# Moving two thirds of the last batch's shared upward products and batch 2's shared downward products behind the expert loop

## The reference, cut to what is computed

```python
router_logits = x @ gate_w.T
topk_w, topk_idx = jax.lax.top_k(softmax(router_logits), 6)      # of 64 experts
h = silu(einsum('th,eih->tei', x, experts_w1))                   # 176 wide
routed_out = sum over a token's 6 experts of weight * (h @ w2.T)
gu = x @ shared_gate_up.T ; g, u = split(gu, 2)                  # 352 wide each
shared_out = (silu(g) * u) @ shared_down.T
x = x + routed_out + shared_out
```

## Time and profile before

| | us |
|---|---|
| median of 3 runs (1401.63 to 1403.54) | 1402.77 |
| the profiled execution's own time | 1403.14 |
| its span | 1401.3 |
| PE busy | 1269.8 (91%) |
| DVE busy | 821.6 (59%) |
| ACT busy | 461.0 (33%) |
| POOL busy | 377.1 (27%) |

### The profile page before, as it was taken

The page is one execution under the profiler, slowest core; times in us unless marked ns, Lnnn a source line. Parts: engine busy times, 40 slices in busy tenths (PEclk is TensorE's granted clock), DMA queues, the critical chain, the costliest instruction groups (busy, mean ns, idle before and its releaser), DMA issues.

```text
span 1401.3 us, 19618 instructions
## 1 busy us (share of the span) xinstructions
PE 1269.8 (91%) x6002; PEld 813.4 (58%) x6002; DVE 821.6 (59%) x2227; ACT 461.0 (33%) x1038; POOL 377.1 (27%) x464
## 2 busy tenths in 40 slices
PE   5499999999999899998999999998177899899988
PEld 4256665555665556556568888886143546455454
DVE  1556776787578957794533333333468665776431
ACT  0255525553345425452211111111142432524310
POOL 0033203253334413361430000002457063330200
PEclk9799999999999999999999999999578999999999
DMA  9999999999800100012158777774222012000000
GB/s 310 413 415 409 410 408 408 409 400 386 335 1 23 69 1 1 8 64 86 62 163 238 224 227 228 229 225 134 68 64 72 1 46 61 23 23 15 1 16 15
DMA packets 107611, 234.40 MB, mean 167 GB/s; under 512 B 12400, under 2 KB 61200, under 8 KB 107152
## 3 DMA queue, kind: packets, MB, share of 16 engines
q1 hardware_dynamic: 80912, 191.50, 37.9%
q0 software_dynamic: 9216, 25.18, 5.6%
q10 hardware_dynamic: 17408, 16.78, 3.5%
HBM read 66.70 MB, written 166.72 MB: 167 GB/s over the span
## 4 chain that ended last, share of the span: by engine, by line
PE 71%; DVE 21%; issue 3%; ACT 2%; POOL 2%; DMA 1%; ACTq 0%; DVEq 0%; POOLq 0%; SPq 0%
PE bank L1234 8%; PE bank L1245 8%; PE bank L537 5%; PE bank L625 4%; PE bank L498 4%; PE bank L499 4%; PE bank L563 4%; PE bank L1476 3%; DVE negmax L839 3%; PE bank L1465 3%; DVE r L850 3%; PE bank L1459 3%; PE bank L546 3%; PE bank L1510 2%; PE bank L1620 2%
## 5 line engine op out<-in xcount | busy, mean ns | idle before, releaser
L697 ACT ACTIVATE r<-bank,negmax 128x128 f32<-128x128 f32 (+3 forms) x256 | 134.9, 527 | 173.8 <-DVE negmax L839 173.4
L537 PE MATMUL bank<-r 128*128 128x512 f32 (+3 forms) x512 | 184.3, 443 | 0.0
L839 DVE TENSOR_REDUCE negmax<-bank 128x1 f32<-128x128 f32 (+3 forms) x256 | 124.0, 485 | 41.5 <-PE bank L538 38.8
L934 POOL TENSOR_TENSOR r<-r,tables 128x256 f32<-128x256 f32 x56 | 42.1, 751 | 328.0 <-ACT r L680 327.8
L546 PE MATMUL bank<-tables,r 128*128 128x128 f32 x640 | 115.1, 278 | 12.2 <-DVE r L850 11.7
L1154 POOL DMA_INDIRECT w2buf<-sent,slots x48 | 49.6, 1034 | 280.5 <-ACTq L1290 258.7
L1234 PE MATMUL bank<-r 128*88 128x256 f32 x512 | 122.8, 383 | 1.9 <-DVE r L1301 1.9
L1146 POOL DMA_INDIRECT sent<-r,slots x96 | 94.0, 979 | 99.7 <-DVE slots L1074 40.0
L1245 PE MATMUL bank<-w2buf,r 88*128 88x256 f32 x512 | 118.5, 379 | 0.0
L546 PEld LDWEIGHTS bank<-tables,r 128*128 128x128 f32 x640 | 72.8, 141 | 66.0 <-DVE r L850 31.7
L1282 ACT ACTIVATE r<-bank 88x512 f32<-88x512 f32 x64 | 37.9, 592 | 219.7 <-PE bank L1234 219.7
(11 more groups left out here) (256 smaller groups left out, 2275.5 us busy)
## 6 DMA issues: line engine op xcount, KB each, us to landing
sent<-gath SPq DMA_DIRECT2D x8, 16384.0 KB, 95.8
r<-sent SPq DMA_DIRECT2D x64, 256.0 KB, 3.2
sent<-r ACTq DMA_DIRECT2D x64, 256.0 KB, 3.2
r<-w1T_dram SPq DMA_DIRECT2D x64, 176.0 KB
w2buf<-w2T_dram SPq DMA_DIRECT2D x64, 176.0 KB
r<-w_o_dram SPq DMA_DIRECT2D x1, 2048.0 KB, 14.2
x<-x_dram SPq DMA_DIRECT2D x1, 2048.0 KB, 19.7
out_dram<-x SPq DMA_DIRECT2D x4, 512.0 KB, 2.9
```

Of the source, the lines that this page charges most:

```text
L537: nc.tensor.matmul(at[:, 0:n], QT[g % 2][:, h, i * P:(i + 1) * P], KT[:, 0:n], start=True, stop=False)
L697: nc.scalar.activation(prob[:, u % 4, 0:(i + 1) * P], bank[SCORE[u % 4]][:, 0:(i + 1) * P], ACT.Exp, bias=negmax[:, u:u + 1], scale=1.0, a ...
L839: nc.vector.tensor_reduce(negmax[:, u:u + 1], bank[SCORE[u % 4]][:, 0:(i + 1) * P], axis=AX.X, op=ALU.max, negate=True).then_inc(A["max"], 1)
```

## The change

On every engine `shared_up/silu/hidden(3, (0, 1))`, `shared_down(2)` and `shared_add(2)` move from in front of the expert loop to behind it. On DVE they stand in front of the six `weigh`. PE gets a wait behind its loop for the last copy of the expert results (`M["ey"]`), since the downward products of batch 2 write banks 4 and 5, and `shared_down(3)` loses its wait on `R["trips"]`, which had come long before.

```diff
             with pe.Fori(0, last_it) as it:
                 step(it, True)
             step(last_it, False)
+            hold(pe, "pe", M["ey"], LT4 * last_it + LT4 + START)
...
             for i in range(TB):
-                if b == BATCH - 1 and i < 2:
-                    pe.wait_ge(R["trips"], 1)
-                else:
+                if b < BATCH - 1 or i >= 2:
                     need(pe, M["sacc"], TB * b + i - 1)
...
             shared_silu(act, 2, (0, 1, 2))
-            shared_silu(act, 3, (0, 1))
             experts_scalar(act)
-            shared_silu(act, 3, (2,))
+            shared_silu(act, 3, (0, 1, 2))
...
             shared_add(dve, 1)
-            shared_hidden(dve, 3, (0, 1))
-            shared_add(dve, 2)
             route.shares(c)
             route.portions(c)
             experts_vector(dve)
+            shared_hidden(dve, 3, (0, 1))
+            shared_add(dve, 2)
             for k in range(TOPK):
                 route.weigh(c, k)
             shared_hidden(dve, 3, (2,))
...
             shared_down(pe, 1)
+            experts_tensor(pe)
             shared_up(pe, 3, (0, 1))
             shared_down(pe, 2)
-            experts_tensor(pe)
             shared_up(pe, 3, (2,))
             shared_down(pe, 3)
```

## The result

The changed kernel takes 1407.82 us (median of 6 runs, 1405.9 to 1409.14) against 1403.62 us (1401.63 to 1404.1, 6 runs) beside it: a ratio of 1.0031, 95% interval 1.002 to 1.0042. It is 4.2 us slower. The profiled execution has a span of 1405.6 us, 4.3 us more than before.

What follows compares the result with a forecast made beforehand. Sends and loads, not PE, set the expert loop's start; behind it POOL's gathers run with 3.1 us of DVE slack. -0.3 + 4.4 + 0.9 = +5.0 us on 1403.14 us, less 0.37 us for the median: 1407.8 us, range 1404.8 to 1411.0 us.

Steps and rivals of the forecast that it cites:

- The front: Before the expert loop: weights limit the gain to 0.6 us, clock costs 0.3 us; -0.3 us, between -1.9 and +0.7.
- Clock at the front: First upward products at the loop's start: PE's idleness costs 0 to 1.3 us more at low clock; 0.3 us taken.
- The loop: Inside the expert loop: nothing added between turns, SP's queue unchanged; zero.
- The new wait: PE behind the loop: waits for the last expert result's copy, until 969.05 us against 968.06 us before; 1.0 us.
- The weighings behind the adds: DVE behind the loop: weighings follow the moved adds, delaying tile 0's return and POOL's third gather group; +4.4 us.
- over 4 us: Sign in the profile after: POOL waits over 4 us for DVE before the third group of gathers.
- Batch 3's downward products: PE behind the loop: first half at low clock, 8.2 us, delays tile 1's return and the fourth gather group; +0.9 us.
- both halves slow: Batch 3's downward products, both halves as slow as before (10.0 us): +2.9 us, used in the clock rival.
- The clock decides: Rival: PE keeps the low clock in both short stretches, in front and behind; +8.0 us, 1410.8 us; chance 0.20.
- Early experts: Rival at PE's loop start: rows could load some 12 us earlier; -6.8 us, 1396 us; chance 0.05.
- Paid back: Rival: front yields its whole 1.92 us wait, clock stays up for batch 3's downward products; +2.5 us, 1405.3 us; chance 0.13.

Runs made afterwards that it cites:

- run 2: Run 1's kernel with DVE's return of tile 0 put ahead of the last chunk's hidden product; ratio 1.0003 to the kernel before.
- Run 3: Kernel before, with DVE's shares and portions ahead of the last batch's hidden products and batch 2's adds, nothing moved behind the loop; ratio 0.9999.
- Run 5: Run 2's kernel with as many unused filler matmuls on PE in front of the loop as were moved away; ratio 0.9999 to the kernel before.
- run 11: Kernel before with portions early and expert weights issued ahead of the wait for the sends, repeated on a chip without stalls; ratio 0.9981.
- run 1: Changed kernel with DVE's six weighings put ahead of the moved hidden products and adds; ratio 1.0002 to the kernel before.
- run 4: Changed kernel with a third gather buffer, so POOL's third group waits for nothing, DVE's order kept; ratio 1.0001 to the kernel before.
- run 8: Run 2's kernel with SP issuing the first four tiles' expert weights before waiting for the sends; ratio 0.9996 to the kernel before.
- run 6: Run 5's kernel with 80 already met waits on PE in place of the filler matmuls; ratio 1.0003 to the kernel before.
- run 12: Run 5's kernel with the weights issued ahead of the wait for the sends, repeated on a chip without stalls; ratio 0.9988 to the kernel before.

## Why the prediction was right, point by point

*The time.* 1407.8 us forecast, 1407.82 us measured. That the two agree so closely is luck. The effect was forecast at +5.0 us and is +4.2 us, since a term of 0.9 us came to nothing, and the kernel before happened to come out 0.85 us higher in the six runs than in the three. What was right is the mechanism: without that term the sum is +4.1 us.

*The front, -0.3 us.* Measured -0.39 us in the profile. Its main reason held: PE's work was hidden (11.78 us of idle time ended by the rows). The weights are what comes last in runs 2 and 3 (1.44 and 1.64 us); in the changed kernel's own trace it is the copy behind the slow transposes (0.83 us), so there the low clock took part of the gain directly. Run 3 shows that even DVE's part of the gain was nearly nothing.

*Clock at the front, 0.3 us.* I took the 3.64 us of the first product for what a short pause always costs. Run 5 had it at 1.96 us after 0.77 and 1.39 us of pauses, run 11 at 3.53 us after 1.02 and 0.76 us, which is less in all. So the length of the pauses alone does not decide it. What does is not shown, and my term was one draw of it.

*The loop, 0.* Held: from the start of the second upward product to the last copy it is 246.51 us (968.75 - 722.24) against 246.44 us.

*The new wait, 1.0 us.* 0.97 us, and it passes on only through DVE's queue: in run 2 PE has the same wait, and POOL waits for nobody.

*The weighings behind the adds, +4.4 us.* This is the step that carries the result. The return of tile 0 ended at 991.65 us (forecast 991.3 us). Measured from the last copy, the third group of gathers starts 4.57 us later than before (991.91 - 968.75 against 986.95 - 968.36). Runs 1, 2 and 4 take it away. But the POOL wait is 3.08 us, less than the "over 4 us" I named, because the first gather was itself 1.9 us late, of which I had nothing. The late store does not add to the 4.57 us, which DVE sets; once POOL hardly waits for DVE any more, in runs 1, 2 and 4, it is what is left.

*Batch 3's downward products, +0.9 us.* Mis-sized: the products took 7.10 us, not 8.2, and the return of tile 1 ended at 996.18 + 3.10 = 999.28 us, just when POOL had finished its third group. POOL's wait there is 0.30 us, the length of its ordinary pause between two gathers. The term is 0. There is also a slip in my sum for both halves slow: 988.2 + 10.0 = 998.2 us, last add 998.6 us, return 1001.7 us against 999.0 us is +2.7 us and not +2.9 us, so the rival of the clock stands at 1410.6 us.

*The rivals.* "The clock decides" did not come: the first product lost to the clock what it had lost before (3.71 and 3.64 us), only the transposes a little more, and the downward products lost less than before. "Early experts" is refuted by the row that ends PE's 11.78 us. "Paid back" lies outside the interval of the ratio by a little (+2.5 us against +2.8 to +5.9).

## What to carry to other kernels

Before moving work from in front of a stretch to behind it, ask on each engine's queue what stands behind it there, and whether that needed anything of it. DVE's weighings needed nothing, and putting them behind a wait for PE used up 3.1 us of slack and then let GpSimd stand still for 3.1 us.

Work under a cover is free where it is; moving it gains nothing until what ends the cover (here the sends, then the rows and weights) comes earlier. Of the kernels here only the kernel before with the weights issued ahead of that wait came out clearly below it (0.9981 and 0.9973, on two chips), with the shared work left where it was; the profile shows 0.95 us of this, the rest is not explained.

## What the runs showed of the hardware that I had not expected

With a 16 KB load of PE's instructions beside it, a 256 KB store landed in 3.7 to 4.0 us instead of 2.15 us (the changed kernel and runs 1, 2, 4 and 8 against runs 3, 5, 6, 11, 12 and before). 80 instructions without work, put in front of the loop, moved the load from 1.9 us behind the last expert copy to 3.5 us ahead of it, and the store was on time again. So a change in the order of a long program can shift a transfer that it never touched.

A return instruction of DVE that usually takes 0.485 us took 2.48 us beside one TENSOR_TENSOR of POOL (1.91 us) and 4.33 us beside two that ran without a gap (3.75 us). In run 1 POOL's second one had to wait 0.71 us for PE, whose four products just before (L1569) took 3.54 us at a granted clock of 0.55 (1064.8 to 1068.4 us), where the kernel before did them in 1.98 us at 1.00. So the slower products went with the shorter stretch.

A wait that is already met, with a semaphore increment, cost PE 0.15 us, 27 us for 176 of them.
